# Summing the weighted values of a group on VectorE instead of folding groups on GpSimd, in a feed-forward, attention, feed-forward kernel

## What is computed

```python
x = x + 0.5 * ffn(layernorm(x))          # first pass
x = x + attention(layernorm(x))
x = x + 0.5 * ffn(layernorm(x))          # second pass, same weights

def ffn(x):                              # ternary weights, one scale per output
    h = silu(lin(x, w1)) * lin(x, w2)    # 256 -> 1024
    h = gelu(lin(h, h1)); h = gelu(lin(h, h2))
    return lin(h, w3)                    # 1024 -> 256

# attention: each row n attends to the rows n - delta, for 24 deltas (20 different ones)
idx = arange(n)[:, None] - deltas[None, :]
scores = einsum('bhnd,bhnod->bhno', q, k_g) * scale + pos_bias
out = einsum('bhno,bhnod->bhnd', softmax(scores), v_g)      # 16 heads of 16
return (out * sigmoid(x @ Wgate + bgate)) @ Wout + bout
```

## Time and profile before

| | |
|---|---|
| median of 3 runs | 1589.89 us (1585.19 to 1591.61) |
| profiled execution, its own time | 1588.57 us |
| its span, first to last instruction | 1586.7 us |
| mean granted TensorE clock | 0.987 of full speed |
| instructions | 19160 |
| subtile period in the trace (values of s0 to values of s15, over 15) | 81.1 us |

### The profile page before, as it was taken

How to read it: one execution, slowest core, us unless ns; L and a number is a source line. 1 busy time by engine, 2 the same in 40 slices (tenths; PEclk the granted TensorE clock), 3 DMA queues, 4 the chain that set the end, 5 groups by cost and what they waited for, 6 DMA issues and landing times.

```text
span 1586.7 us, 19160 instructions
## 1 busy us (share of the span) xinstructions
PE 1498.8 (94%) x6978; PEld 1222.8 (77%) x6978; DVE 1085.1 (68%) x1475; ACT 676.7 (43%) x1062; POOL 553.8 (35%) x402
## 2 busy tenths in 40 slices
PE   7689999999999999999999999999999999998998
PEld 6567888778777778787778877768788877786887
DVE  6323768895777687777876867778676978793322
ACT  7434445353343435354434353434343444352442
POOL 2003051535171607162526070533615245434020
PEclk9899999999999999999999999999999999999999
DMA  8763848666776494857765757557475776754332
GB/s 309 264 225 112 285 143 308 224 210 229 235 243 214 157 316 148 280 178 276 255 231 192 253 180 267 181 194 257 159 263 179 264 247 222 274 202 148 130 98 76
DMA packets 189218, 342.41 MB, mean 216 GB/s; under 512 B 15552, under 2 KB 138560, under 8 KB 188736
## 3 DMA queue, kind: packets, MB, share of 16 engines
q1 hardware_dynamic: 189120, 341.13, 62.7%
HBM read 319.05 MB, written 30.41 MB: 220 GB/s over the span
## 4 chain that ended last, share of the span: by engine, by line
PE 67%; DVE 11%; POOL 8%; DMA 7%; ACT 4%; issue 3%; SPq 0%; DVEq 0%; POOLq 0%; ACTq 0%
PE f_bank L1103 22%; PE f_bank L1104 22%; PE a_banks L1181 6%; PE f_bank L1032 4%; PE f_bank L1033 4%; DMA weights_hi<-in_ffn_w 4%; POOL acc L695 3%; PE f_bank L1132 2%; PE f_bank L1133 2%; DVE slot L937 2%; DVE S L943 2%; DVE slot L981 2%; PE a_banks L1201 2%; POOL acc L692 1%; POOL h_lo L709 1%
## 5 line engine op out<-in xcount | busy, mean ns | idle before, releaser
L1103 PE MATMUL f_bank<-h_hi,wring 128*128 128x512 f32 x2048 | 812.5, 397 | 35.9 <-POOL h_lo L709 13.3
L1104 PE MATMUL f_bank<-h_lo,wring 128*128 128x512 f32 x2048 | 801.7, 391 | 0.0
L1103 PEld LDWEIGHTS f_bank<-h_hi,wring 128*128 128x128 f32 x2048 | 387.1, 189 | 125.0 <-issue 21.3
L1104 PEld LDWEIGHTS f_bank<-h_lo,wring 128*128 128x128 f32 x2048 | 387.0, 189 | 80.8 <-issue 1.4
L775 ACT ACTIVATE h_hi<-f_bank,colv 128x512 fp32r<-128x512 f32 x256 | 176.2, 688 | 532.1 <-PE f_bank L1104 531.8
L897 DVE TENSOR_TENSOR h_lo<-f_bank,h_hi 128x512 fp32r<-128x512 f32 x256 | 174.7, 686 | 242.0 <-ACT f_bank L776 240.9
L709 POOL TENSOR_TENSOR h_lo<-f_gated,h_hi 128x512 fp32r<-128x512 f32 x128 | 165.8, 1308 | 442.9 <-ACT h_hi L769 442.1
L1032 PE MATMUL f_bank<-fT_hi,w_in 128*128 128x512 f32 x480 | 195.6, 408 | 13.6 <-ACT f_gated L764 6.4
L1033 PE MATMUL f_bank<-fT_lo,w_in 128*128 128x512 f32 x480 | 189.2, 394 | 0.0
L981 DVE TENSOR_TENSOR slot<-slot,a_banks 128x1280 f32<-128x1280 f32 (+4 forms) x124 | 169.4, 1375 | 20.4 <-DMA slot<-keys_and_values 20.2
L937 DVE TENSOR_TENSOR slot<-slot,a_banks 128x1280 f32<-128x1280 f32 (+4 forms) x124 | 170.5, 1375 | 18.6 <-DMA slot<-keys_and_values 18.4
(11 more groups left out here) (117 smaller groups left out, 1327.8 us busy)
## 6 DMA issues: line engine op xcount, KB each, us to landing
wring<-weights_hi SPq DMA_DIRECT2D x256, 512.0 KB, 4.7
slot<-keys_and_values SPq DMA_DIRECT2D x128, 384.0 KB, 4.7
slot<-keys_and_values SPq DMA_DIRECT2D x64, 640.0 KB, 4.0
slot<-keys_and_values SPq DMA_DIRECT2D x312, 128.0 KB, 4.5
slot<-keys_and_values SPq DMA_DIRECT2D x64, 256.0 KB, 5.5
weights_hi<-in_ffn_w SPq DMA_DIRECT2D x16, 512.0 KB, 5.1
keys_and_values<-kv_out SPq DMA_DIRECT2D x32, 256.0 KB, 2.3
xf<-in_x SPq DMA_DIRECT2D x8, 512.0 KB, 6.2
```

What stands on the lines that cost most here:

```text
L1103: pe.matmul(bank[:, :], hi, h_hi[src][:, k, :], start=(k == 0), stop=False)
L1104: last = pe.matmul(bank[:, :], hi, h_lo[src][:, k, :], start=False, stop=(not general and k == KH - 1))
```

## The change

The product of weights and values stays where it was. Behind it VectorE now sums the group's offsets itself: one `tensor_reduce` over o of the slot, read as (p, d, o), into one row of 256 per group, `sums[:, n, g, :]`. GpSimd only adds these rows: 0 + 1 into `z`, then 2 and 3 onto it. `acc` and the fold are gone. The slot is free when the sum is done (`a_row`), for the values of block 1 and for the keys of the next subtile. Before the first sum of a subtile VectorE waits until GpSimd's adds of the subtile before have read `sums` (the first block) or `sums` of the block. The numbers of the order are set anew: the values' multiplication is planned at 62.74 instead of 58.4 after the subtile's start, at the same step of 3.1.

```diff
-TIMES = [4.5, 9.5, 11.8, 13.4, 16.0, 24.8, 22, 3.8, 5.6, 53.0, 58.4, 3.1, 87.5, 3.5]
+TIMES = [4.5, 9.5, 11.22, 13.4, 16.0, 24.8, 22, 3.8, 5.6, 53.0, 62.74, 3.1, 87.5, 3.08]
...
-        acc = sb("acc", [P, GS, D])
+
+        sums = sb("sums", [P, SB, 4, D])
...
             def a_v_load(a, n, g):
                 if n == 0 or not in_group[a.c][0][g]:
                     wait_alone(a_qk, qk_done(a, 1, g))
                 else:
-                    wait_alone(a_acc, acc_done(a, 0, g))
+                    wait_alone(a_row, qk_done(a, 0, g))
...
-            def a_add(a, n, g):
+            def a_add_(a, n, g):
 
                 if g == 0:
                     return
-                count, base = in_group[a.c][n][g], per_acc.at(a, acc_ops[a.c][0] if n else 0)
-                pool.wait_ge(a_pv, qk_done(a, n, g))
+                base = per_add.at(a, adds_of[a.c][0] if n else 0)
+                pool.wait_ge(a_row, qk_done(a, n, g))
                 if g == 1:
-                    after(pool, a_acc, base)
-                    pool.tensor_tensor(acc[:, :, :], slots[0][:, :, :], slots[1][:, :, :], ALU.add).then_inc(a_acc, 1)
+                    after(pool, a_zturned, a.at(1, 0))
+                    first = sums[:, n, 0, :]
                 else:
-                    pool.wait_ge(a_acc, base + (g - 1))
-                    pool.tensor_tensor(acc[:, 0:count, :], acc[:, 0:count, :], slots[g][:, 0:count, :], ALU.add)\
-                        .then_inc(a_acc, 1)
...
+                    pool.wait_ge(a_add, base + (g - 1))
+                    first = z[:, n, :]
+                pool.tensor_tensor(z[:, n, :], first, sums[:, n, g, :], ALU.add).then_inc(a_add, 1)
...
                 dve.tensor_tensor(rows_, rows_, weights.unsqueeze(3).to_broadcast([P, count, HEADS, DH]), ALU.mult)\
                     .then_inc(a_pv, 1)
+                dve.wait_ge(a_pv, qk_done(a, n, g))
+                if g == 0:
+
+                    after(dve, a_add, per_add.at(a, 0) - (0 if n else adds_of[a.c - 1][1]))
+                dve.tensor_reduce(sums[:, n, g, :], slots[g][:, 0:count, :].rearrange("p o d -> p d o"), AX.X, ALU.add)\
+                    .then_inc(a_row, 1)
```

More of the change, by code:

```diff
@@ L30 @@
          "z", "out"]
-TIMES = [4.5, 9.5, 11.8, 13.4, 16.0, 24.8, 22, 3.8, 5.6, 53.0, 58.4, 3.1, 87.5, 3.5]
-FOLLOW = dict(silu=-1.5, gate=0.1, cut=1.9, low=2.0, gelu=-0.6,
-              lo=0.9, residual=-1.3, residual2=0.4, fill=20.7, stats=-0.6, turn=4)
-OPENING = dict(block=5.2, block_step=1.8, compare=2.4, done=15.5, step=3.1, turn=8.5)
+TIMES = [4.5, 9.5, 11.22, 13.4, 16.0, 24.8, 22, 3.8, 5.6, 53.0, 62.74, 3.1, 87.5, 3.08]
+FOLLOW = dict(silu=-1.5, gate=0.1, cut=1.9, low=2.26, gelu=-0.6,
+              lo=0.9, residual=-1.3, residual2=0.4, fill=20.83, stats=-1.48, turn=4)
+OPENING = dict(block=5.8, block_step=1.91, compare=2.68, done=15.5, step=3.1, turn=8.13)
 STARTS = [70, 149, 219, 312, 386, 453, 537, 617,
-          688, 768, 847, 925, 1006, 1087, 1158, 1236]
+          688, 768, 847, 925, 1006, 1087, 1160.4, 1234.7]
 class Counts:
@@ L714, in _ @@
             pool.wait_ge(s_const, 16 * 3)
-            schedule({"f_rstd": f_rstd_, "f_low": f_low_, "a_rstd": a_rstd_, "a_bout": a_bout_, "a_add": a_add},
+            schedule({"f_rstd": f_rstd_, "f_low": f_low_, "a_rstd": a_rstd_, "a_bout": a_bout_, "a_add": a_add_},
                      timeline()[0])
```

31 lines of the change are left out of this document (10 added, 21 removed).

## The result

The changed kernel takes 1705.2 us (median of 4 runs, 1702.6 to 1710.0), the kernel before 1588.6 us on the same chip (1585.2 to 1591.6). The ratio is 1.0733, 95% interval 1.0713 to 1.0753: 7.3% slower, 122 us above the forecast of 1583 and far above its range.

The account below looks back on a forecast made before the run. TensorE, busy 94% of the span, was taken as the bound, with only its idle and low-clock time to win or lose. 1588.6 - 37.3 (GpSimd's lateness) + 32.2 (VectorE's) = 1583.5, said as 1583 us; range 1560 to 1608.

Parts of the forecast that it names:

- I take 1.49 us: VectorE's new strided sum over five offsets costs 1.49 us, the lower bound, as the score reduction; upper bound 2.82 us.
- the row of the small product over 16 pieces: Profile row of a product over 16 two-element pieces, 80 bytes apart, 188 ns; taken as showing jumps have no price.
- The first rule that I quoted: Skill page on SBUF: 16-byte lines, fp32 strides freely only up to 4 elements, so every element of the sum would pay.
- the last rival: Strided sum on VectorE runs at half rate, 153 us more, at least half showing: 1660 to 1740 us; chance 0.08.
- The slack of 328 us: VectorE's idle time between 130 and 1460 us, where all attention lies: busy 1002.2 of 1330 us before the change.
- GpSimd's lateness, -37.3 us: TensorE's waits owed to GpSimd, 27.1 us, plus 10.2 us of half clock behind holes; taken as gone in full.
- VectorE's lateness, +32.2 us: New TensorE waits and half clock charged by walking VectorE's new order through 16 places; sum 32.2 us.
- The two worst places: TensorE stands 3.3 us in `f_in` 1 at starts of passes 6 and 11, each with 1.7 us of half clock.
- What comes back: VectorE's moments shorten without waits behind GpSimd's wide adds: one `f_stats` from 6.2 to 2.2 us; VectorE 1230 to 1260 us.
- Bears it better: Rival: only a quarter of the 32 us charged to VectorE comes true, 1560 to 1568 us; chance 0.21.
- GpSimd as late as before: Rival: GpSimd's adds wait for late sums and hold low parts; only clock stretches saved, about 1600 us; chance 0.06.
- The queue is worse than walked: Rival: six more places behind VectorE's pairs pass the 2 us half-clock point, 3.7 us each: 1606 us; chance 0.23.

Follow-up runs that it names:

- experiment 13: Kernel before, VectorE untouched, every GpSimd add cut to one row of 256 (four fifths of the sum left out), old numbers of the order: 1552.95 us.
- experiment 14: Kernel before with GpSimd's adds cut to one row, VectorE untouched, and the new numbers of the order: 1573.42 us.
- experiment 2: Changed kernel with each sum reading five neighbouring elements straight, so wrong elements are added; instructions, bytes and waits stay: 1600.35 us.
- 6: Changed kernel with straight-read sums (wrong elements added) and the old numbers of the order: 1602.74 us.
- Experiment 7: VectorE alone, no kernel computation: sums and products with elements in pairs or fours; product writing fours 1492 ns, sum over 5 separate rows 2311 ns.
- 9: Changed kernel with products written in neighbouring pairs, product and sum made two steps of the order, GpSimd's row planned 1.5 us later: 1619.01 us.
- 11: Changed kernel with paired products, sum as its own step, old numbers, and low part of block (1, 2) planned 1.5 us earlier every pass: 1592.19 us.
- 12: Kernel of 11 with the first half of every pass's residual step also planned 1.2 us earlier: 1596.41 us.

## Why the prediction was wrong

The runs give the change as a sum of single edits, each the difference of two medians. They come from several chips, on which the kernel before lay between 1588.6 and 1591.0 us, so each step is known to some 2 us at best:

| step | us |
|---|---|
| kernel before | 1589.2 |
| GpSimd's adds become one row (13) | -36.3 |
| new numbers of the order (14 less 13) | +20.5 |
| VectorE sums, at the full rate (2 less 14) | +26.9 |
| the sum steps over rows (changed kernel less 2) | +104.9 |
| changed kernel | 1705.2 |

The order of the edits matters for two rows. With GpSimd's adds cut to one row the new numbers cost 20.5 us; under straight sums they change the time by -2.4 (2 less 6). The 20.5 and the 26.9 are therefore sure as a sum, 47.4, and not one by one. The row of 26.9 also holds that GpSimd has 92 adds instead of 188 instructions, and that these wait for the sum and not for the product.

**The step that failed** is "I take 1.49 us" for the strided sum. It measured 2.31 us alone and 2.43 in the kernel, between the two bounds and nearer to the upper one of 2.82. With the sum at 1.49 us the same kernel takes 1600.35 us (experiment 2), inside the recorded range of 1560 to 1608. What carried the choice was the row of the small product over 16 pieces, 188 ns, whose "16 jumps show no price". The row was right and the inference wrong: each of its pieces has two neighbouring elements. Experiment 7 shows that a product that jumps between pairs pays nothing (1493 ns for 1280 elements), while the sum that jumps with every element pays (2311). It was a form of the cheap kind, held as evidence for one of the dear kind.

The first rule that I quoted, of the Trainium skill, SBUF — State Buffer, section Door 1: The DMA port swizzle, spoke for the loss and got too little weight. Its limit of free strides, 4 elements of fp32, isn't what the runs show: for 320 elements a step of 2 takes 486 ns and one of 4 takes 712. The measurement decides: 2 is free, 4 is not, and 3 was not run. A closer rule stands on another page of the Trainium skill, Vector Engine (DVE) Microarchitecture Reference, section 5.2 Measured stream behaviour on trn2: a port keeps its rate while its elements come in runs of at least two adjacent words, and in its table, of a program with two sources, one source that hops 4 KiB with every element costs 1.73 ns per column. The prediction did not weigh it, and it was the rule that spoke against this change. The runs agree on the pairs and nearly on the size (1.67 ns per element). They are milder in two cases: three rows in turn run near the full rate (1032 ns for 768 elements, 953 read straight), and a step of 2 elements at it (486 ns for 320).

**What 0.9 us more per sum did.** In the last rival I wrote that at least half of the added VectorE time would show. VectorE's added time was 101.7 us and the loss 104.9: all of it showed. Between the spans of experiment 2 and of the changed kernel, 103.9 us apart, TensorE's idle time grew from 95.1 to 164.8 us, by 69.7, and its busy time by 34.2, which is clock. The slack of 328 us is an average. In the stretches from a subtile's first product to its last sum there is next to none: in the changed kernel the 16 stretches are 540.9 us long, 33.8 each, and VectorE is busy for 535.2 of them; in experiment 2 they are 446.4 us long, 27.9 each, with 433.4 busy. A pair of 3.8 us stands there for each planned 3.1.

That the time fell inside the last rival's bounds is in part luck. The rival added 153 us to VectorE, of which half to all would show; the runs added 102, and all of it showed. With the measured price its bounds would be 1634 to 1685, and 1705 lies above them: its price was too high and the 1583 beneath it too low, and the two offset each other. Its reason, VectorE as the bound for 1327 of 1330 us, did not come either: VectorE is busy for 1229.9 of the 1440 us between 130 and 1570 us, and it is the bound only in the stretches of the values.

**GpSimd's lateness, -37.3 us:** right. -36.3 us by experiment 13, the half clock included, though its two parts were off against each other: between the spans TensorE's idle time fell by 24.2 us where 27.1 were taken, and its busy time by 12.9 where 10.2 were. One row was misread: the stretch of 6.8 us at half clock begins at 1434.00, while the hole lasts until 1436.43, so only 4.4 us of it are work. GpSimd's 289.1 us against "about 288" is right too.

**VectorE's lateness, +32.2 us:** too small by 15. It stands against 20.5 + 26.9 = 47.4 us. The two worst places came as walked in experiment 2 (3.05 us each at passes 6 and 11, released by L895; the low part of pass 7 with 2.78 at 791.94). The half clock of pass 7 did not come: behind that hole the granted clock is 1.00, where the walk charged 1.7 us. What the walk lacked are places that the new numbers spoil by themselves. I had walked the stretches in which values are multiplied, and given s10 only late gate steps; behind low parts among its score steps 5.6 us stand in experiment 14, with no sum on VectorE at all, where 2.5 stood before. A late `a_z` in s9 (3.70 us at 959.81 in experiment 2) was not walked either; 3.01 us of it are there in experiment 14 too. But the full-rate sum on the old numbers cost 49.8 us (6 less 13): the old numbers were no way out, and the places alone don't explain the 15 us.

**What comes back.** In the changed kernel VectorE's other work is 1085.1 + 275.4 - 1313.1 = 47 us shorter than before. The 1230 to 1260 us of the prediction allow at most 27, and with the sum at full rate VectorE is at 1211.4 (experiment 2), below that range. Experiment 13 measures 33.2 us of it with VectorE's instructions untouched (1085.1 against 1051.9): instructions take longer beside GpSimd's wide adds. Much of it is in the moments; first the kernel before, then experiment 13:

```profile
L808 DVE TENSOR_TENSOR a_mo<-a_st 128x2 f32<-128x2 f32 x16 | 14.4, 903 | 0.6
```

```profile
L808 DVE TENSOR_TENSOR a_mo<-a_st 128x2 f32<-128x2 f32 x16 | 6.1, 379 | 0.6
```

TensorE's own waits for VectorE did not fall by it (20.7 us before, 22.2 in experiment 13). Its waits for `a_hat`, which stands behind the moments and behind GpSimd, fell from 7.4 to 0.8, and how much of that is owed to the moments is not shown.

**The rivals.** "Bears it better" and "GpSimd as late as before" are out (GpSimd's part of the waits fell from 13.3 us to 0.9 in experiment 2). "The queue is worse than walked" would have been the right one with a sum at full rate: 1600 to 1603 us measured, 1606 worked out, with other places than I named. Its point of 2 us for the half clock is no rule either: the clock fell behind a hole of 2.13 us in the kernel before and not behind one of 2.81 in the changed kernel.

**Left open.** How the 26.9 us of the full-rate sum divide over the places isn't measured one by one. Between the traces of experiments 14 and 2 TensorE's waits for `f_gated` and for `xf` rose by 6.2 us each and its busy time by 11.5, while those for `z` and the low parts fell by 3.0 and 0.6. In experiments 9, 11 and 12 each move closed holes and opened others; other moves weren't tried. No version was faster than the kernel before; the best with the sum on VectorE is even with it.

## What to carry to other kernels

Before work is moved to another engine, look at the innermost step of its access, and look for a row of the very same kind: a row with the same number of elements but in neighbouring pairs says nothing on single elements. If a reduction must run across four or more rows, let the instruction that makes its input write it in pairs of neighbours per row; the product took no longer for it here (1377 ns in the mean, 1373 in the changed kernel), and it gave back 104 us. And a table of planned places that is fitted to one version is a cost of its own: change it apart, with the moved work left out, before the two are judged together.

## What the runs showed of the hardware that I had not expected

- A VectorE reduction over rows is nearly at full rate for up to three rows (1.03 us for 768 elements) and jumps with the fourth (1.88 us for 1024, 1.22 read straight).
- Its distance from row to row matters little: 2311 ns at steps of 256, 257, 272, 288, 320 and 384 elements, 2383 at 258, 2419 at 260 and 264; only 500 is dearer, 2736.
- The operands of one product may be cut into different dimensions: read as (offset, head, 16), written as (offset, pair, 2), at the same 1.48 us.
- The strided sum takes 2.31 us alone and 2.43 beside the other engines, 5% more, while the straight one takes 1.486 us in both. What the 5% come from is not shown.
